# A mixer and feed-forward kernel on one core: TensorE's chunk products, three statistics and one root in other places of the order

## The reference, cut to what matters

```python
x = x + layernorm(mixer(layernorm(x)))      # state-space mixer
x = x + layernorm(ffn(layernorm(x)))        # feed-forward

# mixer: 512 inner features, 8 heads of 64, state 64
xi, z = u @ Wx.T, u @ Wz.T
xs = silu(causal_conv(xi, 4 taps))
B, C, dt = xs @ Wb.T, xs @ Wc.T, softplus(xs @ Wdt.T + b_dt)
state = exp(dt * a) * state + (dt * B) outer xs      # per row and head
y = C . state + d * xs
y = group_norm(y, over all rows of the batch and a head's 64 features)
out = (y * silu(z)) @ Wout.T

# ffn: weights binarised, w = mean(|w|) * sign(w)
out = gelu(x @ w1.T + b1) @ w2.T + b2
```

## Time and profile before

| | us |
|---|---|
| median of 3 runs | 1321.09 |
| lowest, highest | 1319.06, 1321.25 |
| the profiled execution, its own time | 1319.61 |
| its span, first to last instruction | 1317.9 |
| PE busy in it | 1228.1 (93%) |
| DVE, ACT, POOL busy | 982.9, 874.9, 492.5 |

### The profile page before, as it was taken

One profiled execution on the slowest core, in us unless ns is written; L12 is line 12 of the kernel. 1 busy time (PEld: TensorE's weight loads), 2 busy tenths in 40 slices (PEclk: granted clock), 3 DMA queues, 4 the chain that ended last, 5 costly groups with the idle time before them and its releaser, 6 DMA issues. The chain is left out here.

```text
span 1317.9 us, 27534 instructions
## 1 busy us (share of the span) xinstructions
PE 1228.1 (93%) x10276; PEld 763.2 (58%) x10276; DVE 982.9 (75%) x2375; ACT 874.9 (66%) x1549; POOL 492.5 (37%) x575
## 2 busy tenths in 40 slices
PE   6989999999999999999999999999999999999675
PEld 4555647565564756556475665647566465755543
DVE  6575886879687777878768787777868777786574
ACT  6565686668766686666866677656876668566443
POOL 2131246143441534324452334414343253522533
PEclk9999999999999999999999999999999999999888
DMA  8020102111020111102011110201112121110100
GB/s 229 1 65 1 34 17 49 33 33 33 17 66 17 34 40 34 40 17 66 16 35 41 22 53 17 65 17 34 33 25 57 17 44 22 18 33 17 33 1 32
DMA packets 91811, 48.07 MB, mean 36 GB/s; under 512 B 63104, under 2 KB 89876, under 8 KB 91680
## 3 DMA queue, kind: packets, MB, share of 16 engines
q1 hardware_dynamic: 91680, 46.33, 15.1%
HBM read 22.72 MB, written 8.39 MB: 24 GB/s over the span
## 5 line engine op out<-in xcount | busy, mean ns | idle before, releaser
L1590 PE MATMUL bank<-sh,WbT 128*128 128x512 f16 x768 | 176.6, 385 | 6.5 <-DVE sh L1218 5.9
L1590 PE MATMUL bank<-sh,WcT 128*128 128x512 f16 x768 | 171.3, 379 | 0.0
L874 POOL TENSOR_TENSOR Cd<-Cd,CT 128x512 f32<-128x512 f32 x64 | 95.1, 1486 | 157.4 <-ACT Cd L1117 157.4
L1780 PE MATMUL bank<-uh,sign1T 128*128 128x512 f16 x512 | 126.8, 384 | 18.1 <-ACT hf L1145 10.8
L1145 ACT ACTIVATE hf<-bank,vectors,alpha 128x512 f32<-128x512 f32 x128 | 99.4, 778 | 63.7 <-DVE hh L1442 40.5
L1213 DVE SCALAR_TENSOR_TENSOR xs<-xi,vectors,xs 128x512 f32<-128x512 f32 x168 | 125.1, 749 | 6.1 <-ACT xs L1022 2.4
L1590 PEld LDWEIGHTS bank<-sh,WbT 128*128 128x128 f16 x768 | 73.5, 99 | 95.7 <-DVE sh L1218 11.1
L1590 PEld LDWEIGHTS bank<-sh,WcT 128*128 128x128 f16 x768 | 75.2, 98 | 86.6
L1793 PE MATMUL bank<-sign2T,hh 128*128 128x256 f16 x1024 | 120.2, 277 | 1.8 <-DVE hh L1442 1.8
L1117 ACT ACTIVATE Cd<-bank 128x512 f32<-128x512 f32 x64 | 38.2, 596 | 122.5 <-PE bank L1688 122.5
L1793 PEld LDWEIGHTS bank<-sign2T,hh 128*128 128x128 f16 x1024 | 100.3, 99 | 17.8 <-DVE hh L1442 2.6
(11 more groups left out here) (218 smaller groups left out, 2688.9 us busy)
## 6 DMA issues: line engine op xcount, KB each, us to landing
xt<-L_attn_input_tensor_dram SPq DMA_DIRECT2D x16, 512.0 KB, 4.2
u<-L_attn_input_tensor_dram SPq DMA_DIRECT2D x16, 512.0 KB, 3.9
out_dram<-u SPq DMA_DIRECT2D x16, 512.0 KB, 3.0
yT<-in_L_ffn_w_dram SPq DMA_DIRECT2D x2, 512.0 KB, 8.8
u<-in_L_ffn_w_dram SPq DMA_DIRECT2D x2, 512.0 KB, 9.2
BT<-in_L_attn_Wx_dram SPq DMA_DIRECT2D x1, 512.0 KB, 5.0
BT<-in_L_attn_Wz_dram SPq DMA_DIRECT2D x1, 512.0 KB, 4.5
zs<-in_L_attn_Wb_dram SPq DMA_DIRECT2D x1, 512.0 KB, 6.3
```

The source lines that it names most:

```text
L874: pool.tensor_tensor(Cd[n % 2][:, :, :], Cd[n % 2][:, :, :], CT[:, :, q * P:(q + 1) * P], ALU.mult)\
L1590: mm = nc.tensor.matmul(bank(t, key)[:, :], w[i][:, k, cols(m)], v[h][:, k, :], start=(a == 0), stop=(a == len(terms) - 1))
L1780: mm = nc.tensor.matmul(bank(t, key)[:, :], sign1T[:, k, cols(f)], uh[i][:, k, :], start=(a == 0), stop=(a == len(terms) - 1))
```

## The change

All of it is in the order of steps, and in which step of the list two of PE's handlers stand for.

- PE's parts of `ends` and `front` get step names of their own, `E` and `seg` (the second with the transposes of x and B); ACT, DVE and POOL keep `ends` and `front`. For chunks 1 to 3 both stand together as before. For chunk 0, `E` stands behind `H` 3 and `seg` behind `H` 5.
- `sums` stands ahead of `H` 0 and not behind `H` 1.
- `in_stat` stands behind chunk 0's `front` and not behind `C` 2.
- `head_stat` 0, 0 (in block 1) stands behind `in_norm` and not behind `C` 2; `head_stat` 1, 0 behind `back` 2 and not ahead of `carry` 2.
- `end_stat` stands behind `score` 3 and not ahead of chunk 3's `ends`; `end_root` behind `carry` 2 and not ahead of `score` 3; `end_norm` behind `carry` 3 and not ahead of `carry` 2. In block 0 `gated` 1, 0 so comes to stand ahead of `end_norm`.

```diff
--- before.py
+++ after.py
@@ -205,29 +205,32 @@
         steps += own(("C", j, 0)) + tail(("uT", j)) + own(("cums", j), ("roles", j), ("skip", j), ("C", j, 1))
         if j == 0:
             steps += weights(("Wout", 0), ("Wout", 1))
-        steps += own(("C", j, 2)) + [(who, "in_stat", nj)] + (own(("head_stat", 0, 0)) if j else [])
+        steps += own(("C", j, 2))
         if j == 0:
             steps += weights(("w2", 0), ("w2", 1))
-        steps += own(("C", j, 3)) + tail(("H", j, 0), ("H", j, 1))
+        steps += own(("C", j, 3), ("sums", j)) + tail(("H", j, 0), ("H", j, 1))
         if j == 0:
             steps += weights(("w2", 2), ("w2", 3), ("alpha2", 0))
-        steps += own(("sums", j)) + tail(*[("H", j, f) for f in range(2, KF)])
+        steps += tail(("H", j, 2), ("H", j, 3)) + own(("E", j, 0)) + tail(("H", j, 4), ("H", j, 5)) + own(("seg", j, 0))
+        steps += tail(("H", j, 6), ("H", j, 7))
 
         norm, xT = [(who, "in_norm", nj)], [(who, "xT", nj), (who, "load", nj)]
-        steps += own(("decays", j), ("ends", j, 0), ("front", j, 0)) + tail(("O", j, 0))
+        steps += own(("decays", j), ("ends", j, 0), ("front", j, 0)) + [(who, "in_stat", nj)] + tail(("O", j, 0))
         if j == 0:
             steps += weights(("w1", 0), ("w1", 1))
-        steps += own(("score", j, 0), ("ends", j, 1), ("front", j, 1))
+        steps += own(("score", j, 0), ("E", j, 1), ("ends", j, 1), ("seg", j, 1), ("front", j, 1))
         if j == 0:
             steps += weights(("w1", 2), ("w1", 3), ("alpha1", 0))
-        steps += own(("score", j, 1), ("carry", j, 0)) + norm + tail(("O", j, 1)) + own(("back", j, 0)) + xT
-        steps += own(("ends", j, 2), ("front", j, 2), ("score", j, 2), ("carry", j, 1), ("back", j, 1)) + tail(("end_stat", j))
-        steps += own(("ends", j, 3), ("front", j, 3)) + tail(("end_root", j)) + own(("score", j, 3))
-        steps += [(who, "xi", nj, 0)] + own(("head_stat", 1, 0)) if j else []
-        steps += tail(("end_norm", j, 0), ("end_norm", j, 1)) + own(("carry", j, 2), ("back", j, 2))
+        steps += own(("score", j, 1), ("carry", j, 0)) + norm + (own(("head_stat", 0, 0)) if j else [])
+        steps += tail(("O", j, 1)) + own(("back", j, 0)) + xT
+        steps += own(("E", j, 2), ("ends", j, 2), ("seg", j, 2), ("front", j, 2), ("score", j, 2), ("carry", j, 1), ("back", j, 1))
+        steps += own(("E", j, 3), ("ends", j, 3), ("seg", j, 3), ("front", j, 3), ("score", j, 3))
+        steps += [(who, "xi", nj, 0)] if j else []
+        steps += tail(("end_stat", j)) + own(("carry", j, 2), ("back", j, 2)) + tail(("end_root", j)) + (own(("head_stat", 1, 0)) if j else [])
         steps += tail(("gated", 1, 0)) if j == 0 else []
         steps += [(who, "conv", nj, 0, 0, 2)] if j else []
-        steps += [(who, "silu_table")] + own(("carry", j, 3), ("back", j, 3))
+        steps += own(("carry", j, 3)) + tail(("end_norm", j, 0), ("end_norm", j, 1))
+        steps += [(who, "silu_table")] + own(("back", j, 3))
         steps += tail(("gated", 1, 1)) if j == 0 else []
         if j == 0:
             steps += weights(("ready", 0))
@@ -407,9 +410,9 @@
 
             if kind in ("xi", "z", "B", "C", "dt", "cums", "sums", "Wo", "H", "O"):
                 return [(kind, *at)]
-            if kind == "front":
+            if kind == "seg":
                 return [*[("seg", *at, g) for g in range(HP)], ("X", *at), ("Bt", *at)]
-            if kind == "ends":
+            if kind == "E":
                 return [("E", *at)]
             if kind == "score":
                 return [("S", *at, g) for g in range(HP)]
@@ -421,7 +424,7 @@
 
         own_keys, tail_keys, in_keys = [], [], []
         for who, kind, *at in turn_steps(False, False):
-            if kind == "ends" and at[1] == 0:
+            if kind == "E" and at[1] == 0:
                 own_keys.append(None)
             turned = kind in ("cums", "sums") or (kind, *at) == ("xi", 0, 0)
             (tail_keys if who == "tail" else in_keys if turned else own_keys).extend(uses(kind, *at))
@@ -1796,7 +1799,7 @@
 
             all_batches(pe, {
                 "weights": weights, "first_turn": first_turn, "xi": project_x, "z": project_z, "dt": step_size, "B": project_b, "C": project_c,
-                "cums": running_sums, "sums": decay_sums, "front": front, "ends": ends, "score": score, "carry": carry, "back": back, "gn_mean": head_means,
+                "cums": running_sums, "sums": decay_sums, "seg": front, "E": ends, "score": score, "carry": carry, "back": back, "gn_mean": head_means,
                 "Wo": attention_out, "uP": turn_middle, "H": hidden, "O": ffn_out})
 
 
```

## The result

The changed kernel takes **1331.55 us** (median of 4 runs, 1331.32 to 1332.88) against 1320.59 of the kernel before (median of 4 runs, 1319.06 to 1321.25): ratio 1.0085, 95% interval 1.0073 to 1.0098. It is 11 us slower; the forecast was 1321.5 with a range up to 1328. The profiled execution has a span of 1329.8 us, 11.9 more than before.

The account below looks back on a forecast made before the run. PE was busy 93% of the span, so only its idle time could be gained. Second blocks -3.4, first blocks +2.1 and opening +1.8 came together to +0.5: 1321.5 us, range 1312 to 1328 (forecast's own 1317.5 to 1325.5).

Parts of the forecast that it names:

- last C product to scores, second block: Feed-forward rows of a second block: first row to chunk 0's scores falls from 15.03 to 13.5 us, -1.5.
- last C product to scores, first block: Feed-forward rows of a first block: 13.66 against 13.76 us, row 0 starting 0.16 later behind the decay sums, -0.1.
- end of a first block: Root's stall replaced by end statistics: PE gains 0.46 at the state but conv starts later, 539.55 against 539.18, +0.4.
- end of a second block: End statistics stand on DVE's gapless path, so the last group statistics and PE's mean product come later, +0.9.
- clock: Rival, chance 0.03: longer mean-product waits halve PE's clock for seven 5 us stretches, 1339; the forecast itself took no cost.
- batch 0: Opening: group statistics come after the state, +1.4 once, and input statistics push the first masks by some +0.4; together +1.8.
- end of the last block: The last block's end comes out even, -0.1.
- The advanced products by themselves are worth nothing: Feed-forward rows: PE work taken from behind row 7 was the cover for its gelu and split; gain 0.
- they end just ahead of the masks' start; nothing is lost: Second block: input statistics behind chunk 0's dt scaling end at 14.0, masks start at 14.7; cost 0.
- The group statistics go into a DVE gap of 2.4 us before the second output tile: Second block's start: the moved first-half group statistics fit DVE's idle time there; no cost given.
- late normalisation: Rival, chance 0.13: ACT's later normalisation, not DVE, sets the block ends, costing 1.6 and 0.9; +8, 1329.
- Block ends hidden: Rival, chance 0.17: ACT and DVE slack hides the block-end costs, so the feed-forward rows' gain stays, about 1312.

Follow-up runs that it names:

- experiment 4: Kernel before with only PE's sums, E and seg of chunk 0 advanced, statistics unmoved: 1320.58 us, ratio 1.0006.
- experiment 12: Changed kernel with the input statistics' two small DVE instructions exchanged, variance plus epsilon first (the swapped kernel): 1331.61 us, one run.
- experiment 1: Changed kernel without its block-end part, so only the start statistics moved and the products advanced: 1316.19 us, ratio 0.9974.
- experiment 3: Kernel before with only input statistics moved behind chunk 0's front and first half's group statistics behind in_norm: 1310.33 us, ratio 0.9927.
- Experiment 10: Experiment 9's kernel plus the advanced products of chunk 0 (sums, E and seg): 1302.58 us, ratio 0.9872 to the kernel before.
- experiment 7: Kernel before with input and first half's group statistics in DVE's idle gap ahead of uT, plus a buffer wait: 1309.86 us, ratio 0.9927.
- experiment 5: Kernel before with only the second half's group statistics moved behind back 2: 1331.1 us, ratio 1.0086.
- experiment 2: Kernel before with only the change's block-end part: 1333.47 us, ratio 1.0106.
- experiments 6: Kernel before with end_root behind back 2 and end_norm behind gated 1, 0, end and group statistics unmoved: 1313.19 us, ratio 0.9951.
- experiment 8: Kernel before with the edits of experiments 3 and 6 together: 1303.28 us, ratio 0.9874.
- experiment 9: Kernel before with the edits of experiments 7 and 6 together: 1301.24 us, ratio 0.986.

## Why the prediction was wrong

The verdict (no change) and the range failed; the picture of which stretches gain and which lose held. Point by point, per block:

| step of the prediction | forecast | measured |
|---|---|---|
| last C product to scores, second block | -1.5 | -1.6 |
| last C product to scores, first block | -0.1 | -0.2 |
| input statistics ahead of the masks (first, second block) | 0 | +0.50, +0.25 |
| end of a first block | +0.4 | +0.7 (-0.51 + 1.19) |
| end of a second block | +0.9 | +1.3 |
| clock | 0 | +0.44 in 3 of 6 |
| batch 0 | +1.8 | +2.7 |
| end of the last block | -0.1 | +0.95 |

- **Right.** The rows: 13.5 forecast, 13.43 measured, with a PE wait of 0.55 inside the output tile (0.8 said). "The advanced products by themselves are worth nothing": experiment 4. PE's gain of 0.46 at the first block's state product was 0.51. Of the signs of wrong and right that were named, conv came 6.07 us after the end normalisation (538.67 to 544.74; 6 said) and the mean's wait was 1.88 (1.5 said).
- **The step "they end just ahead of the masks' start; nothing is lost" failed**, the most instructive error. It had them end at 14.0 and the masks start at 14.7, by adding DVE's durations as they were in their old place. Of those 0.7 us the scaling of the first output tile takes 0.60 (L1454, 516.09 to 516.69), so 0.1 was free. In the new place the negated mean stands beside POOL's `xdw`, and took 0.78 and 0.53 us instead of 0.17, each time ending with `xdw` (515.33 + 0.78 and 515.04 + 1.04; in experiment 12 again). That makes 0.61 and 0.36 of delay, of which the 0.1 takes its part; the transposes behind the scores lose 0.50 and 0.25. Times seven first and six second full blocks this is 5.0 us, nearly half of the miss. The Trainium skill (SBUF — State Buffer, "Who interferes with whom") says that VectorE in a two-port mode, which a scalar operation can enter, and GpSimd exclude each other, and the one that comes second waits for the whole of the first. The trace agrees with the whole wait; that this instruction runs in such a mode, and that it is this port and not another resource, no run here shows.
- **Why experiment 1 is 6 us behind 3.** In 3 the same instruction took 0.91 us beside `xdw` and cost nothing, the stretch stayed 1.94. There PE does the segment products behind row 7, and DVE's last split ends 2.88 us ahead of the scores (505.13 to 508.01). With the products advanced the last split ends 2.13 ahead (508.34 to 510.47), so DVE's queue behind it is 0.75 later against PE, and the held instruction shows. Experiment 10 took the statistics away from there, and the 6 us fell to 1.3. Of the 6 us, 7 x 0.50 + 6 x 0.25 = 5.0 are the transposes' delay; most of the rest is the decay sums ahead of row 0, which put the first row 0.68 us behind the last C product in first blocks instead of 0.51 (7 x 0.17 = 1.2). So the advanced products lose little themselves, but use up the room that the statistics need: two steps that are each priced at nothing weren't nothing together.
- **The term of the first block's end was mis-sized**, +0.37 forecast, +0.68 measured. The chain was the right one: statistics, root, end normalisation, gated half, taps, splits. Conv starts 12.34 us after chunk 3's scores, 11.67 before, forecast 12.04, and that difference of 0.30 is the whole of it. The rows of POOL above show where it is: the root began on time (4.67 us after the scores, 4.69 said), the shift behind it took 0.47 instead of 0.20, beside DVE's two-input splits of y (537.89 to 539.17).
- **The term of the second block's end too**, +0.94 against +1.32. DVE is without a gap from 610.61 to the mean, as forecast; the taps began 6.92 us after chunk 3's scores (6.96 by the prediction's own sum), and then took 2.10 from start to the next start where 1.68 was said, beside POOL's additions of `u`, which now begin at 616.11. Again a duration of the old place.
- **The clock** was a rival at 0.03 in which all seven waits set it off. The truth lay between: behind six waits of 1.80 to 1.88 us it fell in three batches, for some 3.4 and not 5 us, and part was given back later (5.84 to 7.11 from the mean product to the attention product, 7.74 to 6.91 behind it): net +0.44 each, 1.3 in all. Its sign of being right, clock 1.00 from 120 to 1230, could not show this: the view rounds the three drops away.
- **The opening** cost 0.9 more than said, nearly all in batch 0's second block: +0.55 in the X1 stretch, +0.95 from there to chunk 3's scores, +1.1 to the mean. The first two come with the start's statistics (2.46 and 12.96 in experiment 3; 1.91 and 12.00 in the kernel before and in experiment 7), the third with the second half's group statistics (experiment 5 has it alone). The step "The group statistics go into a DVE gap of 2.4 us before the second output tile" has no ground in batch 0, which has no output tile yet: there they stand ahead of the addition of `back` 0, and PE waits for it.

```profile
133.17 1.40 DVE L1355 BATCH_NORM_STATS2 gn_stats<-yT 128x6 f32<-128x256 f32 x4
134.48 0.74 DVE L1348 TENSOR_TENSOR yT<-bank,yT 128x256 f32<-128x256 f32 x2
```

```profile
134.94 0.66 PE L1680 MATMUL bank<-ident,xs 128*128 128x128 f32 x4 [1.05 <-DVE yT L1348]
```

- **The end of the last block** was as forecast up to the attention product, which starts 32.71 us behind chunk 0's scores instead of 33.16. Then its 32 products take 9.82 us instead of 8.82, at a lower granted clock: 0.81 before (first row), 0.73 after. Whether the rest of the 0.95 is the clock too stays open; no run changes it by itself.

```profile
1241.20:1250.10 8.90, 8.82 (x32) 7.19 (x32) 2.46 (x7) 7.94 (x16) 5.52 (x8) 0.81 0.00 0
```

```profile
1251.70:1261.60 9.90, 9.81 (x32) 7.87 (x32) 2.46 (x7) 7.94 (x16) 5.52 (x8) 0.73 0.01 2
```

- **The rivals.** The "late normalisation" rival had the nearest number, 1329, but not the mechanism: in experiment 5 the normalisation was on time, and the mean product was late all the same. "Block ends hidden" is refuted by experiment 2.

Sum of the misses: statistics 5.0, first ends 7 x 0.31 = 2.2, second ends 6 x 0.38 = 2.3, clock 1.3, opening 0.9, last block 1.05, the rows -0.9: 11.8. The forecast sum of 0.5 is rounded up: its own terms for a first block, -0.10 and +0.37, give 1.9 and not 2.1 for seven, and the last block's -0.1 is not in it, so 0.2. Together 12.0, against 11.9 measured. (The 75.5 and 79.7 us that the prediction gives for the two blocks are 76.4 and 79.1 from first row to first row, and a batch repeats to 0.3 us and not to 0.1; nothing was worked out from them.)

What the forecast did not look for is what experiments 6 and 8 found: the change bundles a gain (root late, -6.4; start's statistics moved, -10) with a loss (the late end statistics, which cost 1.33 us in a first block by themselves and in a second block want the gap of the group statistics). With the losing moves and the advanced products left out the kernel takes 1303.28 instead of 1319.57 (experiment 8), and 1301.24 with the start's statistics in DVE's idle gap (experiment 9).

## What to carry to other kernels

A wait on an in-order engine is a place with a size: before moving a step into or out of one, name what fills it now and check that both fit, since here statistics of 1.4 and of 2.1 us wanted one gap of 1.85 us. A duration read at the old place is not the duration at the new one; list what the other engines do beside the new place, above all POOL beside DVE's short single-input instructions. And test the parts of a bundled change one by one: three of them were worth -10.0, -6.4 and +11.5 us by themselves, and the whole was worth +11.0 and not the sum of these, -4.9, since the parts met in the same waits.

## What the runs showed of the hardware

- A VectorE scalar instruction on 128x4 elements waited for the end of a running GpSimd product of 1.04 us and took up to 0.91 us instead of 0.17, whichever of two such instructions stood first. Statistics (`BATCH_NORM_STATS2`, 1.40 for four) beside POOL's `Cd` product in the same trace kept their length.
- Two of VectorE's two-input taps took 2.17 us beside POOL's additions, 1.76 in the place where they were before; POOL's own state scaling took 1.06 us instead of 0.61 beside VectorE's splits.
- The granted clock can fall to the lower of its two levels (1.2 of 2.4 GHz) after a PE wait of 1.8 us, but did so in three of six equal batches. In the swapped kernel, whose waits are the same, it was again three of six, and not the same three; in experiment 2, again with waits of 1.80 us, one of six; in experiment 5, with waits of 1.72 to 1.80, none.
